# A decoder layer on one core: expert weights folded by a second transfer of their last row and GpSimd subtractions, causal zeros by GpSimd selects, and a new job table

## The reference

```
x = LN(x + self_attention(x))             # 16 heads of 8, one shared key and value head
x = LN(x + causal_att(x) + cross_att(x, ctx))  # second attention: causal over x, and over ctx (2, 512, 64); shared output matrix
x = LN(x + moe(x))                        # 8 experts, top 2
# moe: for each expert e
h = x @ W1[e].T + b1[e]; a, b = split(h); g = a * sigmoid(b)
out += (g @ Wo.T + bo) * comb[..., e]
```

## Time and profile before

| | before |
|---|---|
| median of 3 runs | 189.89 us (189.65 to 189.92) |
| the profiled execution's own time | 191.22 us |
| its span (first to last instruction) | 189.5 us |
| PE busy | 172.8 us (91%) |
| DVE busy | 148.8 us (79%) |
| ACT busy | 114.7 us (61%) |
| POOL busy | 40.6 us (21%) |

### The profile page before, as it was taken

One profiled execution on the slowest core, in us unless ns is written; L12 is line 12 of the kernel. 1 busy time (PEld: TensorE's weight loads), 2 busy tenths in 40 slices (PEclk: granted clock), 3 DMA queues, 4 the chain that ended last, 5 costly groups with the idle time before them and its releaser, 6 DMA issues.

```text
span 189.5 us, 5111 instructions
## 1 busy us (share of the span) xinstructions
PE 172.8 (91%) x2037; PEld 93.1 (49%) x2048; DVE 148.8 (79%) x324; ACT 114.7 (61%) x169; POOL 40.6 (21%) x147
## 2 busy tenths in 40 slices
PE   7998897999999989999699999999999999999970
PEld 3654352445342366645445654665667744444440
DVE  7489961697598769998959989959867459989994
ACT  3743299693949688568557671876589633442510
POOL 7165300014000113002100110103343440003224
PEclk9999999999999999999969999999999999999997
DMA  5990000000000000000000000000000000000001
GB/s 141 303 383 24 4 3 0 6 0 3 4 0 0 4 2 3 6 1 3 3 4 3 2 5 5 0 9 7 1 6 3 3 0 0 0 2 0 0 0 55
DMA packets 2984, 4.75 MB, mean 25 GB/s; under 512 B 753, under 2 KB 1489, under 8 KB 2961
## 3 DMA queue, kind: packets, MB, share of 16 engines
q1 hardware_dynamic: 2962, 4.44, 7.1%
HBM read 4.02 MB, written 0.26 MB: 23 GB/s over the span
## 4 chain that ended last, share of the span: by engine, by line
PE 68%; DVE 16%; ACT 9%; issue 4%; POOL 2%; POOLq 0%; DVEq 0%; ACTq 0%
PE t L718 14%; PE y L630 7%; ACT probs L1007 6%; DVE mneg L825 5%; PE t L376 5%; PE w L700 4%; PE t L532 4%; PE t L580 4%; PE y L595 3%; PE y L613 2%; PE t L571 2%; DVE mneg L838 2%; PE t L521 2%; PE t L566 2%; PE t L517 1%
## 5 line engine op out<-in xcount | busy, mean ns | idle before, releaser
L1007 ACT ACTIVATE probs<-t 128x1024 f32<-128x1024 f32 x60 | 58.6, 1028 | 7.5 <-PE t L580 3.3
L838 DVE TENSOR_REDUCE mneg<-t 128x2 f32<-128x1024 f32 x32 | 38.1, 1220 | 6.0 <-PE t L532 5.7
L718 PE MATMUL t<-w1T,x1T 128*128 128x512 f32 x64 | 29.2, 597 | 0.0
L1054 ACT ACTIVATE part_c<-t 128x512 f32<-128x512 f32 x16 | 9.6, 597 | 19.0 <-PE t L718 19.0
L825 DVE TENSOR_REDUCE mneg<-t 128x4 f32<-128x1024 f32 x16 | 18.9, 1217 | 2.5 <-PE t L499 2.4
L1126 POOL CAST mpart<-mneg 128x8 bf16<-128x8 f32 (+1 forms) x13 | 2.7, 208 | 81.4 <-DVE mneg L838 53.2
L630 PE MATMUL y<-probs,v_c 128*32 128x128 f32 x512 | 17.3, 276 | 0.0
L718 PEld LDWEIGHTS t<-w1T,x1T 128*128 128x128 f32 x64 | 11.5, 190 | 11.7 <-issue 11.4
L630 PEld LDWEIGHTS y<-probs,v_c 128*32 128x32 f32 x512 | 13.0, 109 | 2.5 <-issue 1.7
L832 DVE TENSOR_REDUCE mneg<-t 128x4 f32<-128x1024 f32 (+1 forms) x12 | 14.0, 1207 | 0.0
L1012 ACT ACTIVATE y_sb<-y 128x512 f32<-128x512 f32 x12 | 7.2, 602 | 8.7 <-PE y L613 5.4
(11 more groups left out here) (256 smaller groups left out, 300.7 us busy)
## 6 DMA issues: line engine op xcount, KB each, us to landing
w1T<-in_w1T SPq DMA_DIRECT2D x8, 256.0 KB, 8.0
rest<-in_rest SPq DMA_DIRECT2D x1, 772.0 KB, 7.7
bias_row<-in_rows SPq DMA_DIRECT2D x1, 384.0 KB, 6.4
ctx_room<-in_ctx SPq DMA_DIRECT2D x1, 320.0 KB, 5.7
first<-in_first SPq DMA_DIRECT2D x1, 262.5 KB, 2.8
q_stack_C<-mrow_C SPq DMA_DIRECT2D x16, 3.0 KB
out<-rest SPq DMA_DIRECT2D x4, 64.0 KB, 1.6
first<-in_first SPq DMA_DIRECT2D x1, 128.0 KB, 2.7
```

Source lines behind the costliest of these rows:

```text
L718: last = nc.tensor.matmul(o, x2T[:, (2 * b + q) * P:(2 * b + q + 1) * P], w1T[:, e, :], start=True, stop=True)
L838: emptied(V.tensor_reduce(out=dst, in_=o[:].rearrange("p (i k) -> p i k", i=2), axis=AX.X, op=ALU.max, negate=True), ("SC", b, q, p))
L1007: emptied(A.activation(probs[:, n % NPT, :], o[:], ACT.Exp, scale=SCALE), src)
L1054: A.activation(tanh_b[:, n % NTANH], o[:, :, HF:2 * HF], ACT.Tanh, scale=0.5).then_inc(s_tanh, 1)
```

## The change

1. **Fold.** `WM`, `WG`, their copies and the matrix `fold` are gone. SP loads 127 rows of each expert's `w1T` (`w`), and by a second transfer for each expert (`bw`) the last row, repeated over 127 partitions, into spare room (`row_room`: a new tile `last_row`, and tiles that are used later, `gT` and `gated`). POOL subtracts (`ws`, one for each expert, 127 by 512; `wg` for the gate). `b1` goes straight into row 127 near the start (`bb`), behind no wait. Each `ws` waits for both transfers of its expert; the experts' first `F` waits for all eight `ws` and for `b1`.
2. **Causal zeros.** The 24 `mask_k` matmuls are gone; the mask tile too. Instead POOL sets zeros in the probabilities after the exponential (`zB`, one for each `EB`), and `PB` waits for it rather than for the exponential.
3. **Job table.** All five lists are new. The PE list has 55 matmuls in `N` jobs (32 before). On SP the order is `bg bw0 bb bw1 .. bw7 w0 .. w7`, then the shift transfers `m..`.

```diff
     "pool": """
-        ib ov xr om sA00 bs ob sA01 sA10 rA0 xA0 sA11 sC000 sC001 rA1 xA1 sB01 sC011 sC100 sC101 sB11 sC110 rX01 sC111 rX00 gp01
...
+        ib ob ov xr om wg sA00 ws0 ws1 sA01 ws4 ws2 ws6 ws3 ws7 sA10 ws5 rA0 sA11 xA0 sC001 sB01 rA1 xA1 sC010 zB000 zB001 sC100
...
-        fold = sb("fold", [P, P])
+        last_row, gate_row = sb("last_row", [P - 1, 4, 2 * HF]), sb("gate_row", [P, E])
...
+        def row_room(e):
+
+            if e < 4:
+                return last_row[:, e, :]
+            room = gT[0:P - 1, 2 * e - 8:2 * e - 6, :] if e < 6 else gated[e - 6][0:P - 1]
+            return room.rearrange("p n h -> p (n h)")
...
-                    for i in range(2):
-                        diag = o[:, i * 512:(i + 1) * 512].rearrange("p (m k) -> p m k", k=keys)[:, :, q * P:keys]
-                        last = nc.tensor.matmul(diag, ident_bf[:], mask_k[:, 0:len(pairs), :], start=False, stop=True)
                     give(last, job)
...
-                    wait_emptied(pe, ("UB", b, q, n))
+                    pe.wait_ge(s_zeroed, nth[("zB", b, q, n)])
...
-                    give(nc.tensor.matmul(o[:, 0:E if kind == "WG" else 2 * HF], fold[:], source, start=True, stop=True), job)
...
                     if once("experts"):
-                        pe.wait_ge(s_b1, 16)
+                        pe.wait_ge(s_less, E)
...
-                    emptied(A.activation(dst, o[:, 0:E if kind == "cWG" else 2 * HF], ACT.Copy), src)
...
+                elif kind == "ws":
+                    pool.wait_ge(ld_w1[b], 32)
+                    G.tensor_tensor(w1T[0:P - 1, b, :], w1T[0:P - 1, b, :], row_room(b), ALU.subtract).then_inc(s_less, 1)
+                elif kind == "wg":
+                    pool.wait_ge(ld_rest, 16)
+                    pool.wait_ge(ld_gate, 16)
+                    G.tensor_tensor(w_gT, w_gT, gate_row[:], ALU.subtract).then_inc(s_gate_w, 1)
+                elif kind == "zB":
+                    _, b, q, n = job
+                    wait_emptied(pool, ("UB", b, q, n))
+                    keys = (q + 1) * P
+                    diag = probs[:, unit_of[("EB", b, q, n)] % NPT, :].rearrange("p (m k) -> p m k", k=keys)[:, :, q * P:keys]
+                    G.affine_select(out=diag, in_=diag, compare_op=ALU.is_ge, fill=0.0, base=0,
+                                    pattern=[[0, 1024 // keys], [1, P]], channel_multiplier=-1).then_inc(s_zeroed, 1)
...
-                    sp.dma_start(w1T[:, b, :], packs["w1T"][:, b * 2 * HF:(b + 1) * 2 * HF]).then_inc(ld_w1[b], 16)
+                    sp.dma_start(w1T[0:P - 1, b, :], packs["w1T"][0:P - 1, b * 2 * HF:(b + 1) * 2 * HF]).then_inc(ld_w1[b], 16)
+                elif kind == "bw":
+                    sp.dma_start(row_room(b),
+                                 packs["w1T"][P - 1, b * 2 * HF:(b + 1) * 2 * HF].partition_broadcast(P - 1)).then_inc(ld_w1[b], 16)
```

More of the change, by code:

```diff
@@ L39 @@
     "pe": """
[L40 to L47, removed]
@@ new lines @@
+        VC1:w0 SA02:t2 SA03:t1 N1:y KC0:w0 SA01:t0 SA04:t1 DKC01 SA07:t2 N1:y SA06:t0 DKC02 TA00:t1 N1:y SA05:t0 RKA1:w0
+        RKC10:t1 N1:y RKC11:t2 KC1:w0 SA14:t0 SA12:t2 UA00:t1 DKC11 UA01:t0 TA01:t1 SA11:t2 SA13:t1 DKC12 SA10:t2 SA16:t0
+        UA02:t1 VC0:w0 UA03:t0 UA04:t1 N1:y UA05:t2 PA000 PA001 UA06:t1 UA07:t2 RKC00:t0 TA10:w0 N2:y RKC01:t1 PA010 PA011
+        UA10:t0 UA11:t1 YA00:w0 YA01:t2 UA12:t0 N1:w0 UA13:t1 ZA0:w0 SA17:t2 SA15:t0 WA0:w0 PA100 PA101 RKC30:t2 RKC31:t1 N1:w0
+        RKC20:t0 N2:w0 XA0:w0 RKC21:t2 JV0:w0 JQC0:t1 N1:y TA11:t0 JKB0:t2 JQB0:w0 N5:y RQC00:t2 RQC01:t1 UA14:t0 N2:w0 SC005:t1
@@ L86 @@
-        st10 st01 st11""",
+        bg bw0 bb bw1 bw2 bw3 bw4 bw5 bw6 bw7 w0 w1 w2 w3 w4 w5 w6 w7 mA00 mA01 mA10 mA11 mC001 mC000 mB01 mB00 mC010 mC011
+        mC101 mC100 mB10 mC111 mC110 mB11 st01 st10 st00 st11""",
 }
@@ L565, in _ @@
                                 c0 = i * 512 + m * keys + kt * P
-                                nc.tensor.matmul(o[:, c0:c0 + P], k_stack_b[half(i, KROW), p, q0 + kt * P:q0 + (kt + 1) * P],
+                                last = nc.tensor.matmul(o[:, c0:c0 + P], k_stack_b[half(i, KROW), p, q0 + kt * P:q0 + (kt + 1) * P],
                                                  q_stack["B"][half(i, KROW), p, q0 + q * P:q0 + (q + 1) * P],
-                                                 start=(m == 0 and kt == 0), stop=False)
-                    for i in range(2):
-                        diag = o[:, i * 512:(i + 1) * 512].rearrange("p (m k) -> p m k", k=keys)[:, :, q * P:keys]
-                        last = nc.tensor.matmul(diag, ident_bf[:], mask_k[:, 0:len(pairs), :], start=False, stop=True)
+                                                 start=(m == 0 and kt == 0), stop=(m == len(pairs) - 1 and kt == q))
                     give(last, job)
@@ L688, in _ @@
                     give(nc.tensor.transpose(o[:, 0:P], x2[:, 2 * b + q, :], ident[:]), job)
-                elif kind in ("WM", "WG"):
-                    if once("fold"):
-                        pe.wait_ge(s_fold, 1)
-                    if kind == "WG":
-                        if once("rest"):
-                            pe.wait_ge(ld_rest, 16)
-                        source = w_gT
-                    else:
-                        pe.wait_ge(ld_w1[b], 16)
-                        source = w1T[:, b, :]
-                    o = take(slot, job)
-                    give(nc.tensor.matmul(o[:, 0:E if kind == "WG" else 2 * HF], fold[:], source, start=True, stop=True), job)
                 elif kind == "GL":
                     _, b, q = job
-                    if once("WG"):
-                        wait_emptied(pe, ("WG",))
+                    if once("gate"):
+                        pe.wait_ge(s_gate_w, 1)
                     o = take(slot, job)
```

110 lines of the change are left out of this document (49 added, 61 removed).

## The result

The changed kernel takes **343.73 us** as a median of four executions (343.40 to 344.13), against 189.89 us: a ratio of 1.811 (1.808 to 1.814). The forecast was 335 us, 320 to 352. The profiled execution took 344.0 us for a span of 342.3 us.

A forecast was written before the change was run, and what follows sets the result against it. PE, full from 51.4 us, was taken to bound the kernel now. Shift transfers landing at 174.1 us behind the weights, plus 165.7 for the rest, less 6.0 gained, plus 1.0 cold clock, gave 334.8 us span, about 335 us; range 320 to 352.

The forecast's parts named there:

- One engine for 127 rows: Weight loads: each of the 16 new transfers of 127 rows runs on one DMA engine, the same for all; 163.6 us together.
- The first rival: Weight loads: nearly equal shares, or another engine each time; loads over by 21 or 26 us, 183.9 or 186 us; chance 0.12.
- A transfer takes 10.2 us: Weight loads: 127 rows of 2048 bytes on one engine, at 80.5 ns a row, take 10.2 us.
- the begin at 9.5 us: Weight loads: the 127-row transfers begin when their engine is through with `rest`, taken as 9.5 us.
- It has issued all by 14 us: SP's queue: 18 issues take about 10.6 us, so SP isn't the limit and has issued all by 14 us.
- POOL as second wait: POOL's list: `sA01` stands behind `ws1` (`w1` at 112 us), `sA10` behind `ws7`, which waits for the last weight at 174 us.
- The second rival: Shift transfers on other engines: `UA00` to `UA03` run at 24 us, POOL decides, `UA10` at 181; 329 us median; chance 0.08.
- The subtraction 1.3 us, the selects 0.7 and 1.2: POOL's new work: 1.3 us per 127 x 512 subtraction; selects of 512 and 1024 columns 0.7 and 1.2, costed at nothing.
- Gain of the rest, 6.0 of 7.7 us: From `UA00` on: PE is spared 13.0 us, fillers add 5.3, net 7.7; 6.0 counted as gained, some going to DVE waits.
- Cold clock, 1.0 us: PE after 150 us of rest: clock at its lower level for the first few us, costing 1.0 us.
- Sum: Whole kernel: 174.1 + 165.7 - 6.0 + 1.0 = 334.8 us of span.
- added 0.4 in all: From span to median: plus 1.7 us for execution over span, less 1.3 for median below that execution; about 335 us.

## Why the prediction was right, and where its numbers were off

- **One engine for 127 rows**: right, and shown: one completion for each transfer, 6.6% of 16 engines, 25 GB/s; and 128 rows instead of 127 take 159 us away. The first rival, nearly equal shares, was wrong, though its 183.9 us is near what the same kernel does with transfers that are spread (184.75 us).
- **A transfer takes 10.2 us**: 10.46 from one landing to the next (10.42 is the length of an issue), so a row takes 82.4 ns, not 80.5. Over sixteen that is 3.8 us, and with it the begin at 9.5 us and the landing come out within 0.1 us: `UA00` came at 177.97 us, not 174.1: +3.9.
- **"It has issued all by 14 us"**: this step is wrong. SP issued the last weights at 158.2 us and `mA00` from 158.24 us. The number survived because the shift transfers landed behind the weights either way. I had them issued at 20 us and waiting in an engine's queue; in truth they were not issued, and only the last 9.2 us of their wait (168.71 to 177.92 us) lay in an engine, behind the weights. That the number came out all the same is luck. The run from ACT's queue adds that it is SP's queue that counts: with the same weights in transfer, shift transfers issued by ACT landed within 4.5 us.
- **POOL as second wait**: right. With the shift transfers free, POOL's `sA10` holds the kernel to 337 us. The second rival had the mechanism of that run, but not of this kernel. Its price of 329 us was 8 us too low: `UA10` ran at 188.66 us, not 181, as the weights landed 4 us later and the way from `sA10` to it took 9.1 us, not some 6. It also let `UA00` to `UA03` run at 24 us, where `UA02` and `UA03` stand behind `sA01`'s transpose. From `UA10` on it took 146.7 us, as priced (147).
- **The subtraction 1.3 us, the selects 0.7 and 1.2**: 1.26, and 0.63 to 0.66 for 512 columns and up to 1.27 for 1024. The selects made PE's weight loads wait twice, 0.5 us in all; costed at nothing, that is near enough on this table.
- **Gain of the rest, 6.0 of 7.7 us**: with a warm clock the rest takes 158.0 us, 165.7 before: 7.7 us are there. Mis-sized by -1.7. That it is just the 7.7 of my sum is partly luck. The sum set 23 fillers against the relief, but behind `UA00` there are 29 more (45, and 16 before), so that it should have been 6.3 by its own prices. PE is busy 6.4 us less behind `UA00` (145.8 and 152.2 us) and 2.5 us more ahead of it (23.2 and 20.6): part of the gain is work that was moved there. And the 165.7 are of an execution 1.3 us above the median.
- **Cold clock, 1.0 us**: mis-sized the most. PE stayed at the lower level for 15.5 us, not "the first few", and the rest took 6.3 us longer: +5.3.
- **Sum**: 334.8 + 3.9 - 1.7 + 5.3 = 342.3 us, the span measured. The median is 1.4 above it, where I had added 0.4 in all, from before's execution.

What I did not see is that the relief of PE is bound up with its clock. The gain of 5.1 us with 128 rows shows only on the new table with its fillers (1.2 us or less are left without them); neither part of the change brings it on the old one, where the two together were not run. And with the new table `UA00` is at 25.1 us, not 23.8, which takes 1.3 of the 7.7 us back; the profiled execution of before was itself 1.3 us above its median.

## What to carry to other kernels

Count the rows of a transfer before its bytes: 127 rows cost as much on one engine as sixteen times that on sixteen, and the cure is one row more (overwrite it later) or a split into numbers that divide well. Look who stands behind the slow transfer, on the issuing queue as on the engine that waits for the data: here both held the same work, and freeing one alone gave almost nothing. Before taking work off an engine that is full, look whether its clock stays up without it; here a rest of 3 us put it at its lower level for more than 10 us, and without the fold's matmuls or without fillers the kernel was slower, not faster. And before putting work on an idle engine, look what stands behind it there: two selects ahead of one split made the whole kernel 1.7 us later.

## What the hardware showed that I had not expected

- **SP is held in the issue.** An issue of 127 rows took 10.42 us (0.5 us with 128 rows). In three kernels SP ran about the same number of transfers ahead: 19.4 us at 10.46 us each (after), 19.4 us with half of them (issued by 80.4, landed 99.8), and 9.2 us at 4.95 us for a pair of 118 and 9 rows (issued by 46.8, `UA00` at 56.0; POOL's subtractions there begin at 21.02 and 25.97 us): each time 1.9. What holds SP is not in the profile.
- **The lower clock outlasts the rest.** After 3 us without PE work the granted clock was 0.50 from some 179 to 190 us, with PE busy for 3.8 of every 4 us; after 153 us of rest it was so for 15.5 us. In these runs the cost hardly depended on how long the rest was: 5.3 us after 3 us, 6.3 us after 153.
